# The score mask moved from a TensorE matmul to an add on VectorE, in place in the PSUM bank

## The reference, cut to what matters

```
mask = (it < jb) | (it > jb + w) | (jb == -1)
sim = jnp.einsum('bhwie,bhwje->bhwij', bq, bk2) * QK_SCALE
sim = jnp.where(mask, -jnp.finfo(sim.dtype).max, sim)
attn = jax.nn.softmax(sim, -1)
out = jnp.einsum('bhwij,bhwje->bhwie', attn, bv2)
```

## Time and profile before

| | before |
|---|---|
| median of three runs | 3696.93 us |
| profiled execution | 3698.82 us (span 3697.0 us) |
| TensorE matmuls busy | 3426.7 us, 93% |
| VectorE busy | 2640.4 us, 71% |
| ScalarE busy | 2508.1 us, 68% |
| GpSimd busy | 2356.0 us, 64% |
| mean granted TensorE clock | 0.975 |

### The profile page before, as it was taken

One profiled execution on the slowest core, in us unless ns is written; L12 is line 12 of the kernel. 1 busy time (PEld: TensorE's weight loads), 2 busy tenths in 40 slices (PEclk: granted clock), 3 DMA queues, 4 the chain that ended last, 5 costly groups with the idle time before them and its releaser, 6 DMA issues.

```text
span 3697.0 us, 132440 instructions
## 1 busy us (share of the span) xinstructions
PE 3426.7 (93%) x50548; PEld 2640.8 (71%) x50548; DVE 2640.4 (71%) x5823; ACT 2508.1 (68%) x5117; POOL 2356.0 (64%) x1568
## 2 busy tenths in 40 slices
PE   5666999999999999999999999999999999999997
PEld 4444877777777777777777777777777777777774
DVE  3445877777877777877777877777877777877773
ACT  2224766677777777777777776777776777777774
POOL 1004866667767667767667766667766667767662
PEclk9888999999999999999999999999999999999998
DMA  2000111121111121111121111121111121111111
GB/s 79 0 0 12 48 37 44 37 63 41 50 36 44 39 61 43 47 36 44 41 59 44 47 36 44 39 61 43 47 36 44 41 59 44 47 36 44 41 39 44
DMA packets 98169, 156.71 MB, mean 42 GB/s; under 512 B 18129, under 2 KB 39633, under 8 KB 96721
## 3 DMA queue, kind: packets, MB, share of 16 engines
q1 hardware_dynamic: 93440, 132.73, 13.3%
q10 hardware_dynamic: 4176, 15.74, 1.3%
HBM read 20.48 MB, written 2.10 MB: 6 GB/s over the span
## 4 chain that ended last, share of the span: by engine, by line
PE 77%; issue 6%; ACT 5%; POOL 1%; DVE 1%; ACTq 0%; DMA 0%; DVEq 0%; POOLq 0%; SPq 0%
PE psum L736 19%; PE psum L760 11%; PE psum L826 9%; PE psum L846 7%; PE psum L783 6%; PE psum L803 4%; PE psum L791 4%; PE psum L866 4%; PE psum L878 3%; PE psum L871 3%; PE psum L755 2%; PE psum L857 1%; PE psum L853 1%; ACT probT L553 1%; ACT aoT L510 1%
## 5 line engine op out<-in xcount | busy, mean ns | idle before, releaser
L377 POOL TENSOR_TENSOR qkr<-qks,rnorm 128x1024 f32<-128x1024 f32 x384 | 731.3, 1904 | 371.0 <-issue 291.1
L369 POOL TENSOR_TENSOR qks<-work 128x1024 f32<-128x1024 f32 x384 | 908.0, 2365 | 72.1 <-DVE work L1042 67.8
L385 POOL TENSOR_TENSOR probn<-prob,psumr 128x512 f32<-128x512 f32 x384 | 400.5, 1043 | 506.4 <-DVE psumr L1068 506.4
L536 ACT ACTIVATE sq<-psum 128x512 f32<-128x512 f32 x768 | 463.9, 604 | 346.9 <-PE psum L736 346.3
L736 PE MATMUL psum<-whi,xhi 128*128 128x512 f32 x1152 | 565.1, 491 | 107.0 <-issue 67.2
L1016 DVE TENSOR_REDUCE ssq<-sq 128x8 f32<-128x512 f32 x768 | 515.6, 679 | 48.6 <-ACT sq L536 12.2
L1040 DVE TENSOR_TENSOR work<-psum,rot 128x512 f32<-128x512 f32 x768 | 507.4, 661 | 58.6 <-POOL qks L369 43.3
L1074 DVE TENSOR_REDUCE nmax<-psum 128x8 f32<-128x512 f32 x384 | 264.9, 690 | 335.9 <-PE psum L760 334.6
L760 PEld LDWEIGHTS psum<-kT,qbd 128*64 128x64 f32 x12288 | 403.8, 142 | 109.9 <-issue 109.9
L760 PE MATMUL psum<-kT,qbd 128*64 128x64 f32 x12288 | 458.6, 230 | 0.9 <-issue 0.8
L736 PE MATMUL psum<-whi,xlo 128*128 128x512 f32 x1152 | 458.7, 398 | 0.0
(11 more groups left out here) (131 smaller groups left out, 6490.3 us busy)
## 6 DMA issues: line engine op xcount, KB each, us to landing
vsh<-vtok SPq DMA_DIRECT2D x384, 192.0 KB, 2.5
vsh<-vtok SPq DMA_DIRECT2D x384, 64.0 KB, 3.1
xsh<-xs_in SPq DMA_DIRECT2D x192, 64.0 KB, 2.0
ff_x<-x_mid SPq DMA_DIRECT2D x96, 128.0 KB
wqkv<-Wqkv_dram ACTq DMA_DIRECT2D x5, 1536.0 KB, 7.7
wo_next<-Wo_dram ACTq DMA_DIRECT2D x5, 512.0 KB, 8.3
xtok<-x_dram SPq DMA_DIRECT2D x4, 512.0 KB, 11.0
out_dram<-qkr SPq DMA_DIRECT2D x8, 256.0 KB, 2.5
```

The lines of the kernel that those rows point to most:

```text
L369: pool.tensor_tensor(qks[:, :, :], rcos, rsin, ALU.add).then_inc(s["add_ready"], 1)
L377: pool.tensor_tensor(qkr[:, j % 2, :, :], qks[:, :, :], rnorm[:, :].unsqueeze(2).to_broadcast([P, 2 * OCT, DH]), ALU.mult).then_inc(s["qkr ...
L385: pool.tensor_tensor(probn[:, :, :], prob[:, j % 2, :, :], psumr[:, j % 2, 1, :].unsqueeze(2).to_broadcast([P, OCT, KEYS]), ALU.mult).then ...
L536: act.activation(sq[:, w * OCT:(w + 1) * OCT, :], bank[w].rearrange("p (h n) -> p h n", n=DH), ACT.Square).then_inc(s[("sqq_ready", "sqk_r ...
```

## The change

TensorE no longer issues the mask matmul. The score matmuls start their output instead of adding to it, and the unit's entry of the mask is chosen on VectorE's side. VectorE, ahead of the row maximum, waits for the scores, adds the mask to bank 3 in place (one `tensor_tensor`, 128 x 512, scores and result in PSUM, the bf16 mask from SBUF, repeated over four head pairs), and then waits for this add with a new semaphore, `masked_ready`, before the row maximum. The wait for the scores now goes through `wait_apart`, which moves the value to a register and waits against that. The one wait for `mask_ready` moves from TensorE to VectorE, ahead of the layers.

```diff
-                        need(pe, "sub_ready", units, j, first)
-                        entry = 1 if ti or j < 0 else (it % 2 if isinstance(it, int) else pe.snap(it % 2))
-                        m = mask[:, bass.ds(entry, 1), :, :].rearrange("p a b k -> p a (b k)").to_broadcast([P, PAIRS, 2 * KEYS])
-                        pe.matmul(bank[3].rearrange("p (a k) -> p a k", a=PAIRS), ident_bf[:, :], m,
-                                  start=True, stop=False, skip_group_check=True)
+                        need(pe, "sub_ready", units, j, first)
...
-                                               start=False, stop=(a == PAIRS - 1 and w >= 2), skip_group_check=True)
+                                               start=True, stop=True)
...
                     def row_maximum(j):
                         if j is None:
                             return
-                        need(dve, "sim_ready", units, j + 1)
+                        entry = 1 if j // UPT % TPI or j < 0 else (it % 2 if isinstance(it, int) else dve.snap(it % 2))
+                        wait_apart(dve, ("sim_ready", units + (j + 1)))
+                        dve.tensor_tensor(bank[3].rearrange("p (a k) -> p a k", a=PAIRS),
+                                          bank[3].rearrange("p (a k) -> p a k", a=PAIRS),
+                                          mask[:, bass.ds(entry, 1), :, :].rearrange("p a b k -> p a (b k)").to_broadcast([P, PAIRS, 2 * KEYS]),
+                                          ALU.add).then_inc(s["masked_ready"], 1)
+                        need(dve, "masked_ready", units, j + 1)
                         dve.tensor_reduce(nmax[:, :], bank[3].rearrange("p (a k) -> p a k", k=KEYS), AX.X, ALU.max,
                                           negate=True).then_inc(s["max_ready"], 1)
```

More of the change, by code:

```diff
@@ L182, in build @@
             wqkv_in wo_in w1_in w2_in
-            sqq_ready sqk_ready ssq_ready ssk_ready sg_ready ln_ready rn_ready rotq_ready rotk_ready add_ready qkr_ready trq_ready trk_ready
+            sqq_ready sqk_ready ssq_ready ssk_ready sg_ready ln_ready rn_ready rotq_ready rotk_ready add_ready qkr_ready trq_ready trk_ready masked_ready
             q_ready qk_ready sim_ready max_ready sub_ready p_ready pt_ready pts_ready vp_ready vs_ready pv_ready
@@ L749, in scores @@
                             return
-                        ti, tp, oc = j // UPT % TPI, j // UPT % 2, j % UPT
+                        tp, oc = j // UPT % 2, j % UPT
                         need(pe, "qk_ready", units, j + 1)
                         need(pe, "sub_ready", units, j, first)
-                        entry = 1 if ti or j < 0 else (it % 2 if isinstance(it, int) else pe.snap(it % 2))
-                        m = mask[:, bass.ds(entry, 1), :, :].rearrange("p a b k -> p a (b k)").to_broadcast([P, PAIRS, 2 * KEYS])
-                        pe.matmul(bank[3].rearrange("p (a k) -> p a k", a=PAIRS), ident_bf[:, :], m,
-                                  start=True, stop=False, skip_group_check=True)
                         for a in range(PAIRS):
@@ L899, in attention @@
                 sweep(pe, body)
-            pe.wait_ge(s["mask_ready"], 10)
             pe.wait_ge(s["pad_ready"], 1)
@@ L1122, in _ @@
             dve.wait_ge(s["const_in"], 16 * 2)
+            dve.wait_ge(s["mask_ready"], 10)
             attention()
```

## The result

The change made the kernel slower: 3740.77 us, median of 4 runs (3735.18 to 3742.51), against 3697.66 us (3695.18 to 3699.65, 4 runs) before. The ratio is 1.0114, with an interval of 1.0097 to 1.0132. The forecast was 3650, with a range of 3606 to 3700 and a chance of 0.15 for slower.

A forecast was written before the change was run, and what follows sets the result against it. TensorE, busy 93% of the span, was taken as the bound. Savings of 24 x 1.30 + 15 x 0.5 + 9 x 0.98 = 47 us from 3698.82 gave 3652, less 1.9 for the median: 3650, range 3606 to 3700.

The forecast's parts named there:

- What TensorE saves: One mask matmul in each of 384 units: 0.23 us each, 88 us in all, with 0.31 us as upper end.
- What VectorE pays: A 128 x 512 add per unit ahead of the row maximum, taken as 0.73 us with its hand-over.
- second rival: VectorE becomes the bound and the kernel slower, with an add of 1.07 us or more; 3731 at 1.3 us; chance 0.15.
- The stalls at steps 7 and 1: TensorE waits because `guarded` on VectorE ends late behind the scores: 0.57 us at step 7, 0.19 at step 1.
- L7: How far VectorE's `guarded` ends behind the end of the scores in step 7: 0.97 us, of which 0.40 is free.
- the hand-over's 0.05 us: Extra time where VectorE already stands waiting for the scores, from the register wait: 0.05 us (0 to 0.2).
- Step 2 to 3 ... no stall: VectorE's lateness behind the scores in step 3 is 0.14 us, under the free 0.40, so TensorE doesn't stop.
- let VectorE catch up: Steps 7 to 0, 1 to 2, 3 to 4, 5 to 6 (7.7 us and more) hold VectorE's 6.3 to 6.4 + 0.73 us.
- first rival: All of the saving is kept, as VectorE's free lateness is near 1 us: 3609 us; chance 0.15.
- the 1.84: TensorE's saving per turn from the removed mask matmuls, if nothing gives it back: 8 x 0.23 = 1.84 us.
- a plain turn: A turn without a loop jump: forecast to lose 0.86 of 1.84 us at stalls and hand-overs and keep 0.98.
- These turns keep 1.30: The 24 turns with TensorE's 2.8 us stop at a loop jump each save 1.84 + 0.08 - 0.62 = 1.30 us.

The follow-up runs named there:

- the move: GpSimd's `ffn_normed` moved from the head of step 4 into step 3, ahead of `normed`, in the changed kernel with 160 empty instructions: 3668.79 us (0.9911).
- place 80: Inner loop head at instruction count 80 modulo 256: kernel before with 68 empty instructions, 3684.44 us; changed kernel with 160, 3674.73 us.
- place 12: Inner loop head at instruction count 12 modulo 256: kernel before as it is, 3697.66 us; changed kernel with 92 empty instructions, 3688.63 us.

## Why the prediction was wrong

**What TensorE saves: right.** From the last projection matmul to the scores, in the timeline after:

```profile
2012.87 0.40 PE L736 MATMUL psum<-whi,xlo 128*128 128x512 f32 x1
2013.19 1.15 PE L756 MATMUL psum<-kT,qbd 128*64 128x64 f32 x32
```

0.32 us against 0.55: 0.23 is saved. By starts the projections themselves are 0.24 apart, so some 0.08 us stays ahead of the scores. This fits the drain at a change of tiling mode in the Trainium skill ("TensorEngine Tiling (Array Packing)", Key Properties); no run separates it from another cost of the change.

**What VectorE pays: right.** Its timeline after, step 7 and the next:

```profile
2038.37 0.18 DVE L1020 TENSOR_REDUCE ssg<-ssq 128x16 f32<-128x32 f32 x1
2038.47 0.70 DVE L1070 TENSOR_TENSOR psum<-psum,mask 128x512 f32<-128x512 f32 x1
2039.20 0.69 DVE L1075 TENSOR_REDUCE nmax<-psum 128x8 f32<-128x512 f32 x1
...
2046.03 0.70 DVE L1070 TENSOR_TENSOR psum<-psum,mask 128x512 f32<-128x512 f32 x1 [0.76 <-PE psum L756]
```

The row maximum starts 0.73 us behind the add, the value taken. The add, which writes PSUM, takes 0.70 us, as the operations that only read it (0.69), so the second rival's mechanism, an add of 1.07 us or more, did not happen, though its sign did.

**The stalls at steps 7 and 1: right.** `turn_q`, which follows the scores, starts here at 2037.66 and `turn_k` at 2040.20:

```profile
2037.66 0.66 PE L779 MATMUL psum<-ident,qkr 128*128 128x128 f32 x4
...
2040.20 0.66 PE L787 MATMUL psum<-ident,qkr 128*128 128x128 f32 x4
```

`guarded` ends at 2038.37 + 0.18 = 2038.55, so L7 = 0.89 (0.97 forecast), and the step from 7 to 0 lost 8.19 - (7.93 - 0.23) = 0.49 us (0.62 forecast; the prediction counts the hand-over's 0.05 us twice, in L and again on top of the stalls, so its own reading gives 0.57). The one from 1 to 2 lost 7.93 - (7.89 - 0.23) = 0.27 (0.24 forecast, 0.19 without the second count). The chain shows the way there, `guarded`, ScalarE, `turn_k`:

```profile
2388.92 0.10 DVE ssg L1020
...
2389.05 0.22 ACT lnss L517
...
2390.01 0.60 ACT qbd L546
...
2390.65 0.66 PE psum L787 x4
```

**"Step 2 to 3 ... no stall", and the long steps "let VectorE catch up": half right.** The distance from step 2 to 3 is 6.74 us, no stall. But I looked only at the way from VectorE over ScalarE to TensorE. The way from VectorE over GpSimd to the FFN's `ff_n` costs 0.65 us in the step from 3 to 4. The first rival rightly fell on this side as well: all of the 1.84 is kept not even without an add. Of the 0.65, 0.42 is GpSimd's order, shown by the move; the other 0.23 stays without any add; I put it to ScalarE's order, which no run tests. With 0.08 in step 5 to 6, a plain turn keeps 0.34, where I said 0.98.

**"These turns keep 1.30": the step that failed.** I counted 24 turns with a jump, took their stop of 2.8 us and the clock behind it as a fixed price, and carried both over unchanged. The 20 in layers 1 to 5 became 2.95 us longer: 4.25 us off in each, 85 us in all, which is nearly the whole distance from forecast to result (3650 to 3741). The 4 to a new layer add 10 and the 4 of layer 0 give 7 back. What the runs show in its place is a price that depends on where the heads lie: the same program moved by a number of empty instructions goes from 3741 to 3675 us, and the kernel before from 3698 to 3778. Even at equal places the jump turns keep less than I said: 69.61 to 68.81 us at place 80, 69.92 to 70.02 at place 12.

With the inner head's place held, the change is a gain of 16 and 21 us from the first FFN up to the last, 0.4 to 0.6%; at a plain turn's 0.34, 48 turns would give 16 us. That is a third to under a half of the 47 forecast. The kernel at those places, 3688.63 and 3674.73 us, lies inside 3606 to 3700, and which place a build gets is luck: the forecast held nothing that chooses it.

**What stays open.** Why the cost goes up and down with the place as it does: one law for all three loops doesn't fit (a new layer's jump costs 7 us at place 132, the inner one 3.4 at 112, layer 0's 3.1 at 116). Where the program itself starts within a block isn't known, nor what the three kinds of jump do besides. Whether the end of the loop body, which moves with its length, counts as well as its head was not tested.

## What to carry to other kernels

In a kernel whose program jumps, an edit that adds or removes instructions on the bounding engine moves every loop head behind it, and that alone can be worth more than the edit: split the turns into those with and without a jump before explaining anything, and compare both kernels with the heads at the same place. When the change is done, try a few paddings ahead of the loop; here 128 empty instructions were worth 18 and 23 us over 160 and 192. They are not free: 164 at the head of the program cost 7 us. And where an engine gets more work, follow each of its consumers to the bounding engine, not only the one that was late before: here the second way, over GpSimd, cost 0.65 us a turn, more than the first stall's 0.49.

## What the runs showed of the hardware

The mean price of the same jump back in the inner loop ran, over the runs here, from 2.7 us with its target at place 80 to 6.9 us at place 176, and for the jump to a new layer from 3.4 to 9.9 us. In the kernel before alone it was 3.3 us at place 80 and 6.7 at 176. The dear inner jumps have a second stop a few matmuls behind the first, 1.35 and 1.22 us in the two shown, 3.6 us the longest of any jump, and a longer stretch at the lower clock level behind it (6.7 us a jump against 1.9): the scores take 1.76 us for 28 of them, where all 32 take 1.08 at the cheap place. Between the best and the worst placing seen the kernel before spans 3684 to 3778 us, 2.6%, with no work changed. And VectorE adds into PSUM in place in 0.697 us for 128 x 512, and the operations that only read there take 0.69.
